# Second projection with half of its value columns last, and the cached values of batch 0 gathered during it

## The reference, cut to what matters

```python
q = einsum('bsd,ed->bse', x, Wq)         # 32 heads of 128
k = einsum('bsd,ed->bse', x, Wk)         # 8 heads of 128
v = einsum('bsd,ed->bse', x, Wv)         # 8 heads of 128
q, k = rope(rmsnorm(q, q_norm_w), pos), rope(rmsnorm(k, k_norm_w), pos)
kc = k_cache[block_table]; vc = v_cache[block_table]   # 512 cached positions for each batch
k_all = concatenate([kc, k], axis=1); v_all = concatenate([vc, v], axis=1)
scores = einsum('bqhd,bkhd->bhqk', q, repeat(k_all)) * SCALE     # masked by cache_seqlens
o = einsum('bhqk,bkhd->bqhd', softmax(scores), repeat(v_all))
return einsum('bse,de->bsd', o, Wo)
```

## Time and profile before

| | |
|---|---|
| median of 3 runs | 1663.63 us (1663.25 to 1664.19) |
| profiled execution, its own time | 1663.88 us |
| span of the profiled execution | 1662.1 us |
| mean granted TensorE clock | 0.992 |
| busy share of the span: PE, DVE, ACT, POOL | 97%, 67%, 57%, 18% |
| second projection, first matmul | 553.85 us |
| cached attention, first matmul | 860.17 us |
| all DMAs issued by POOL (queue q0) | 9216 packets, 67.11 MB |
| all DMAs issued by SP (queue q1) | 220826 packets, 222.90 MB |

### The profile page before, as it was taken

The page is one execution under the profiler, slowest core; times in us unless marked ns, Lnnn a source line. Parts: engine busy times, 40 slices in busy tenths (PEclk is TensorE's granted clock), DMA queues, the critical chain, the costliest instruction groups (busy, mean ns, idle before and its releaser), DMA issues. The chain is left out here.

```text
span 1662.1 us, 33975 instructions
## 1 busy us (share of the span) xinstructions
PE 1604.7 (97%) x10728; PEld 1399.0 (84%) x10728; DVE 1112.0 (67%) x2941; ACT 939.8 (57%) x2392; POOL 303.4 (18%) x306
## 2 busy tenths in 40 slices
PE   2899999999999999999989999999999999999998
PEld 2787888888888788888868999999999999977777
DVE  8404543554346557777777999999999999864443
ACT  3224323232322246676667999999999999822221
POOL 1000000000000146565530211211211211022210
PEclk9999999999999999999989999999999999999999
DMA  6621222202210324434558999999999999595401
GB/s 230 210 96 48 71 70 69 69 0 69 69 63 26 127 100 133 125 117 133 158 176 279 301 321 311 297 324 310 296 325 310 300 318 310 186 316 151 120 7 51
DMA packets 230095, 290.69 MB, mean 175 GB/s; under 512 B 17658, under 2 KB 181914, under 8 KB 221850
## 3 DMA queue, kind: packets, MB, share of 16 engines
q1 hardware_dynamic: 220826, 222.90, 42.7%
q0 software_dynamic: 9216, 67.11, 11.2%
HBM read 237.44 MB, written 50.41 MB: 173 GB/s over the span
## 5 line engine op out<-in xcount | busy, mean ns | idle before, releaser
L1607 PE MATMUL p_val<-probs_t,vals 128*128 128x128 f32 x2048 | 272.2, 276 | 0.3 <-DMA vals<-in_v_pages,rows_now 0.3
L1607 PEld LDWEIGHTS p_val<-probs_t,vals 128*128 128x128 f32 x2048 | 249.5, 192 | 0.7 <-DMA vals<-in_v_pages,rows_now 0.7
L1516 DVE CUSTOM_DVE_ANT_0 probs<-p_score,mask 128x544 f32<-128x544 f32 x256 | 184.3, 720 | 41.9 <-issue 35.8
L1420 ACT ACTIVATE probs<-probs,low 128x544 f32<-128x544 f32 x256 | 190.2, 743 | 0.3 <-DVE low L1516 0.3
L1505 DVE TENSOR_TENSOR wo_lo<-keys,wo_hi 128x544 fp32r<-128x544 f32 x224 | 161.8, 722 | 0.6 <-ACT wo_hi L1415 0.6
L459 PE MATMUL p_tile<-w_hi,y_hi 128*128 128x512 f32 x384 | 157.3, 410 | 2.4 <-PEq L472 2.4
L1428 ACT ACTIVATE probs_t<-p_turn 128x512 f32<-128x512 f32 x256 | 148.9, 582 | 17.4 <-PE p_turn L1586 17.3
L1073 POOL TENSOR_TENSOR w_lo<-w_raw,w_hi 128x512 fp32r<-128x512 f32 x44 | 57.7, 1317 | 550.2 <-DVE w_hi L1111 533.9
L1415 ACT ACTIVATE wo_hi<-keys 128x544 fp32r<-128x544 f32 x224 | 145.8, 651 | 18.2 <-PE p_score L461 17.0
L1586 PE MATMUL p_turn<-cst,probs 128*128 128x128 f32 x1024 | 154.7, 274 | 0.2 <-ACT probs_t L1428 0.2
L459 PE MATMUL p_score<-wo_hi,q_hi 128*128 128x272 f32 x448 | 150.9, 337 | 0.8 <-DVE low L1516 0.4
(11 more groups left out here) (218 smaller groups left out, 3541.7 us busy)
## 6 DMA issues: line engine op xcount, KB each, us to landing
keys<-in_k_pages SPq DMA_DIRECT2D x512, 128.0 KB
qk_new<-x_res SPq DMA_DIRECT2D x80, 256.0 KB, 2.2
x_res<-qk_new SPq DMA_DIRECT2D x32, 512.0 KB
o_new<-x_res SPq DMA_DIRECT2D x32, 512.0 KB, 6.5
w_raw<-in_w_vkq_t SPq DMA_DIRECT2D x12, 1024.0 KB, 5.6
w_raw<-in_w_qkv_t SPq DMA_DIRECT2D x10, 1024.0 KB, 8.4
toep<-kpad SPq DMA_DIRECT2D x32, 256.0 KB, 4.5
w_raw<-in_w_dense_t SPq DMA_DIRECT2D x8, 1024.0 KB, 5.4
```

The lines of the kernel that those rows point to most:

```text
L1420: nc.scalar.activation(probs[:, i % 8, :], probs[:, i % 8, :], ACT.Exp, bias=low[:, i % 4:i % 4 + 1], scale=-1.0, accum_out=total[:, i % 4 ...
L1516: v.tensor_tensor_reduce(out=probs[:, i % 8, :], in0=score_at(i % 2, slice(0, KEYS)), in1=mask[:, i // HK, :], scale=1.0, scalar=3e38, op0 ...
L1607: mm = pe.matmul(p_val[:, h, half * P:(half + 1) * P], vals[:, slot, c // RUN, c % RUN * HK * D + k * D:c % RUN * HK * D + (k + 1) * D], p ...
```

## The change

The weight columns are put in another order: the first half of the values, then keys, queries, and the second half of the values last. So pair 0 is 8 tiles of values and 8 of keys, pairs 1 to 4 hold keys and queries, and pair 5 is 8 tiles of queries and 8 of values. The last three turns now stand between tiles of values. DVE makes the page rows after the angles instead of ahead of them, and the tables for the keys ahead of those for the queries. The cached values of batch 0 get a buffer of their own, `vals_0`, at the other end of SBUF, where nothing of `cached_qkv` lies (`v_out` moves there too), and POOL gathers them ahead of the last pair. SP no longer waits at the end of `cached_qkv` for the stores of the values; it waits for them in `cached_attention`, ahead of its first load of `vals_new`. The diff, cut to its core:

```diff
+    def place_values(self, ctx, nc):
+
+        self.vals_0 = ctx.enter_context(nc.sbuf_tensor("vals_0", [P, GATHERS, RUN * HK * D], F32, side="right"))
+    def gather_values(self, pool, to, slot, done, v_pages):
+
+        v_flat = v_pages.rearrange("o (t r) n -> (o t) (r n)", r=RUN)
+        for n in range(GATHERS):
+            pool.indirect_dma_start(to[:, n, :], None, v_flat, bass.IndirectOffsetOnAxis(ap=self.rows_now[:, slot, n:n + 1], axis=0)).then_inc(done, 16)
...
-        pairs = lambda body, eng: (body(1, True, False), _loop(eng, 2, PAIRS - 1, lambda m: body(m, False, False)),
-                                   body(PAIRS - 1, False, True))
+        TURNED = (QKV_CHUNKS - 2) * TT
+
+        pairs = lambda body, eng: (body(0, True, False), body(1, False, False),
+                                   _loop(eng, 2, PAIRS - 1, lambda m: body(m, False, False)), body(PAIRS - 1, False, True))
+        values = lambda i, first, last: first and i < TT or last and i >= TT
...
+            def store_values(w, i):
+
+                sp.wait_ge(tile_taken, w // TT * TURNED + w + 1)
+                sp.dma_start(v_rows[:, i % TT, w // TT * E:(w // TT + 1) * E], v_out[:, i % 2, :]).then_inc(v_stored[i % 2], 16)
...
+                late = [TT - LAG + i // 2 if i % 2 == 0 else TT + i // 2 for i in range(2 * LAG)]
+                order = [*range(TT - LAG), *late, *range(TT + LAG, PAIR)] if last else range(PAIR)
...
+                    if values(i, first, last):
+                        store_values(i, i)
...
-                    if last and i == TT + 3:
+                    if last and i == 3:
...
-            for i in range(2):
-                sp.wait_ge(v_stored[i], 16 * PAIR // 2)
...
+            def take_values(w, i):
+
+                if w == TT:
+                    act.wait_ge(tile_taken, TT + TURNED)
+                if w >= 2:
+                    act.wait_ge(v_stored[i % 2], 16 * (w // 2))
+                nc.scalar.activation(v_out[:, i % 2, :], p_tile[:, i % 4, :], ACT.Copy).then_inc(tile_taken, 1)
...
+                    if first and i == EC:
+                        act.wait_ge(angles3, 1)
+                        nc.scalar.activation(ang[:, :, :, :], ang[:, :, :, :], ACT.Sin).then_inc(sines3, 1)
                     act.wait_ge(tile_done, m * PAIR + i + 1)
+                    if values(i, first, last):
+                        if last and i - LAG < TT:
+                            put(m, i - LAG)
+                        take_values(i, i)
+                        continue
...
             pairs(body, act)
-            for i in range(PAIR - LAG, PAIR):
-                put(PAIRS - 1, i)
...
+            tables.gather_values(pool, tables.vals_0, 0, tables.vals_gathered_0, io["v_pages"])
             tiles(PAIRS - 1, False, True)
-            rotate(PAIRS - 1, PAIR - 1)
...
-            tables.make_rows(v, cst)
...
+            tables.make_rows(v, cst)
...
-            for which in range(2):
+            for which in (1, 0):
...
+                    if not values(i, first, last):
+                        scale_and_rotate(m, i, 1 if first or isinstance(m, int) and m == 1 and i < TT else 0)
...
-            for i in range(PAIR):
-                project(0, i)
-
             def body(m, first, last):
                 for i in range(PAIR):
                     project(m, i)
-                    if i >= LAG:
+                    if i >= LAG and not values(i - LAG, first, last):
                         turn(m, i - LAG)
-                    elif not first:
+                    elif i < LAG and not first:
                         turn(m - 1, PAIR + i - LAG)
 
-            body(1, True, False)
-            _loop(pe, 2, PAIRS, lambda m: body(m, False, False))
-            for i in range(PAIR - LAG, PAIR):
-                turn(PAIRS - 1, i)
+            pairs(body, pe)
...
-        vals = sb("vals", [P, 2, GATHERS, RUN * HK * D])
+        vals = (tables.vals_0, sb("vals_1", [P, GATHERS, RUN * HK * D]))
...
+                    if first and slot == 0:
+                        for i in range(2):
+                            sp.wait_ge(tables.v_stored[i], 16 * TT)
...
+                    if first and slot == 0:
+                        continue
...
-        "w_vkq_t": lay(np.concatenate([inputs["L0_cond2_Wv"], inputs["L0_cond2_Wk"], inputs["L0_cond2_Wq"]]).T),
+        "w_vkq_t": lay(np.concatenate([wv[:E], inputs["L0_cond2_Wk"], inputs["L0_cond2_Wq"], wv[E:]]).T),
...
+            tables.place_out(ctx, nc)
+            tables.place_values(ctx, nc)
```

More of the change, by code:

```diff
@@ L874, in __init__ @@
         self.qk_stored = [sem(f"qk_stored{i}") for i in range(4)]
+        self.v_stored = [sem(f"v3_stored{i}") for i in range(2)]
         self.pages_ready = sem("pages_ready")
@@ L959, in cached_qkv @@
         tile_taken = sem("tile_taken")
-        v_stored = [sem(f"v3_stored{i}") for i in range(2)]
+        v_stored = tables.v_stored
         squares_ready = sem("squares_ready")
@@ L1060, in body @@
                         put(m - 1, PAIR + i - LAG)
-                    if 1 <= i % TT <= EC and not (last and i >= TT):
+                    if 1 <= i % TT <= EC:
                         split_hi(2 * m + 1 + i // TT, (1 + i // TT) % 2, i % TT - 1)
             pairs(body, act)
-            for i in range(PAIR - LAG, PAIR):
-                put(PAIRS - 1, i)
         @block.gpsimd
@@ L1074, in split_lo @@
                                         ALU.subtract).then_inc(lo_piece, 1)
[L1076 to L1078 removed]
+            for c in range(EC):
+                split_lo(1, 1, c)
             def rotate(m, i):
@@ L1087, in tiles @@
                 for i in range(PAIR):
-                    if i >= 1:
+                    if 1 <= i <= TT and not first or i > TT and not last:
                         rotate(m, i - 1)
-                    elif not first:
+                    elif i == 0 and not first:
                         rotate(m - 1, PAIR - 1)
-                    if 1 <= i % TT <= EC and not (last and i >= TT):
+                    if 1 <= i % TT <= EC and not values(i, first, last):
                         split_lo(2 * m + 1 + i // TT, (1 + i // TT) % 2, i % TT - 1)
-            tiles(1, True, False)
+            tiles(0, True, False)
+            tiles(1, False, False)
             _loop(pool, 2, PAIRS - 1, lambda m: tiles(m, False, False))
@@ L1155, in scale_and_rotate, with tiles @@
                 ins.then_inc(tile_taken, 1)
-            def tiles(m, key):
+            def tiles(m, first, last):
                 for i in range(PAIR):
-                    scale_and_rotate(m, i, key)
-            for c in range(EC):
-                split_hi(2, 0, c)
-            tiles(1, 1)
-            _loop(v, 2, PAIRS, lambda m: tiles(m, 0))
+                    if not values(i, first, last):
+                        scale_and_rotate(m, i, 1 if first or isinstance(m, int) and m == 1 and i < TT else 0)
+            pairs(tiles, v)
         @block.tensor
@@ L1279, in cached_attention @@
         v_new_in = [sem(f"v_new_in{i}") for i in range(2)]
-        vals_gathered = [sem(f"vals_gathered{i}") for i in range(2)]
+        vals_gathered = (tables.vals_gathered_0, sem("vals_gathered1"))
         carrier_ready = sem("carrier_ready")
@@ L1378, in body @@
                     b = 2 * m + slot
+                    if first and slot == 0:
+                        continue
                     if not first:
                         pool.wait_ge(val_done, (b - 1) * HK)
-                    if not (first and slot == 0):
-                        row = pool.snap(b) if not first else b
-                        if not first:
-                            hold_wait(0)
-                        nc.gpsimd.tensor_copy(rows_now[:, slot, :], rows[:, bass.ds(row, 1), :].rearrange("p o n -> p (o n)")).then_inc(rows_placed, 1)
-                        pool.wait_ge(rows_placed, b + 1)
-                        hold_wait(1)
-                    for n in range(GATHERS):
-                        gather(vals[:, slot, n, :], rows_now[:, slot, n:n + 1], v_flat, vals_gathered[slot])
+                    row = pool.snap(b) if not first else b
+                    if not first:
+                        hold_wait(0)
+                    nc.gpsimd.tensor_copy(rows_now[:, slot, :], rows[:, bass.ds(row, 1), :].rearrange("p o n -> p (o n)")).then_inc(rows_placed, 1)
+                    pool.wait_ge(rows_placed, b + 1)
+                    hold_wait(1)
+                    tables.gather_values(pool, vals[slot], slot, vals_gathered[slot], v_pages)
             body(0, True)
```

59 lines of the change are left out of this document (21 added, 38 removed).

## The result

The median of the runs fell from 1663.91 to 1652.28 us (four runs each, one more of the kernel before than in its table): a ratio of 0.9935, interval 0.9924 to 0.9947. I had forecast 1654.0. In the profiles the span went from 1662.1 to 1650.1 us, PE's busy time from 1604.7 to 1598.4.

What follows compares the result with a forecast made beforehand. The prediction took PE's own work to bound the kernel, with losses at the second projection's end, the key wait and the clock; 3.9 + 3.7 + 2.9 - 0.9 = 9.6 us less gave 1654.0 us, range 1652 to 1657.

Steps and rivals of the forecast that it cites:

- The end of the second projection: Last four turns move between tiles of values, so the attention starts at 856.25 instead of 860.17: 3.9 us less.
- The weights: Last chunk's weight load lands late beside batch 0's gathers; ACT is 5.0 us late and PE waits 0.9 us.
- The 88% and the 0.3 us: By the skill's packet rule gathers take some 88% of the DMA; the weight load lands about 0.3 us later still.
- The stage's start: Second projection's start: tables needed sooner, ready near 577.8, with 5.7 us to spare; costed at nothing.
- The keys of batch 1: In the attention, keys land 1.4 us ahead of PE, so PE's key wait goes: 3.7 us less.
- a key wait of some us is left: Sign that the forecast is wrong: PE still waits some us for batch 1's keys.
- the margin of 1.4 us: Batch 1's keys land at 874.7, 1.4 us ahead of PE, which is ready at 876.1.
- Rival (2): Batch 1's keys come over 4 us later than worked out, the key wait stays: 1660.6 us; chance 0.17.
- The clock behind the wait: Batch 1 of the attention takes its steady length at full clock: 2.9 us less, or nothing if the wait stays.
- Rival (1): The clock holds through the attention's first rows, winning 2.0 us more: 1652.0 us; chance 0.10.
- The sum: Whole kernel: 3.9 + 3.7 + 2.9 - 0.9 = 9.6 us less, a median of 1654.0 us.

Runs made afterwards that it cites:

- second profile: The changed kernel run once more, unedited, beside three variants on the same chip: 1652.10 us, ratio 0.9941.
- the kernel with later gathers: The changed kernel, but POOL issues batch 1's gathers only when batch 1's keys have landed: 1649.47 us, ratio 0.992.
- the gather alone: The kernel before, old order of tiles, with batch 0's values gathered in the second projection into a buffer at SBUF's other end: 1656.09 us, ratio 0.9966.
- the later set: Runs of the unedited changed kernel again beside three variants on the same chip: 1652.10 us, ratio 0.9941.
- the kernel with the earlier gathers: The changed kernel, but POOL issues batch 0's two gathers one tile (3.2 us) sooner: 1652.02 us, ratio 0.9934.
- the order alone: The changed kernel, but POOL gathers batch 0's values at the attention's start again, ahead of batch 1's: 1658.25 us, ratio 0.9974.

## Why the prediction was right

- **The end of the second projection, 3.9 us.** Right, and a little short: 4.3 at equal clock. The 5.24 of the two profiles holds also the 1.6 us of the clock at 554, which I had not thought could differ behind the same code, less 0.64 by which the changed kernel's profile came to the second projection later.
- **The weights, -0.9.** Wrong in size: nothing. The step that failed is "Beside the gathers SP's queue moves 0.074 x 7.4 = 0.55 MB": it has the load and the gathers start to flow together, near 807 us in the times of before, 2.6 us after their issue. In the changed kernel the load's data came 1.9 us after its issue and the gathers' 4.6 after theirs, when the load was nearly through. The mechanism itself is real, and so is its cover: one tile earlier the load stands still and ACT waits 3.9 us, with no wait on PE. The 88% and the 0.3 us that I set beside this took SP's mean packet of 1.0 KB for the load's. The load's packets are 2.0 KB (0.33 MB in 163), and the same working then gives 78%, about the row's 79%.
- **The stage's start, nothing.** Right: PE has no wait there, and DVE had 4.3 us to spare (5.7 by my working).
- **The keys of batch 1, 3.7 us.** Mis-sized: 2.4 won, 1.33 (1.94 in the second profile) left, which by my own sign, "a key wait of some us is left", is where I was wrong. My time for the landing was near: 18.45 us after the start by my working, 18.82 and 19.40 measured. In part that is luck: from 858 to 867 the gathers moved their 2.10 MB, and so were through some 12 us after the start where I had 10.45, but SP's queue moved 0.88 MB beside them where I had 0.40. What failed is the other side of "the margin of 1.4 us": PE was ready after 17.49 us, not 19.83, because its first rows ran faster. A gain on one side of a wait had used up the margin on the other. Rival (2) did not come true: the keys landed 0.4 and 0.95 us later than I had worked out, not over 4. The gathers of batch 1 held them up by 3.0 to 3.6 us, as the kernel with later gathers shows, and my working had that in it.
- **The clock behind the wait, 2.9 us.** 2.06 won, where I had nothing if a wait stayed. The clock is at 1.00 in this batch, behind a wait of 1.33 us, but that wait costs 18.81 - 18.02 = 0.8 us more in the rows behind it, as the kernel without it shows.
- **Rival (1), the clock in the first rows.** This came true in good part, 2.34 us (I had given it 2.0, and a chance of 0.10). With the gather alone, in the old order, PE is ready for batch 1 after 19.17 us, 0.66 sooner than before, so the order's clock is the other 1.7. It was not won on top, as the rival had it: with the gather alone batches 0 and 1 gain 6.74 us, with the whole change 6.81, since PE was ready sooner only to wait for the keys. The time came out nearer to the rival's 1652.0 than to 1654.0, but not by its path. My reason against it, that 2.4 us of idle time at 554 had brought 0.72, was a poor one, since the same place shows 1.00 in six of the ten profiles. The half clock still comes, but some 2 us after the first scores (0.50 from 857 to 860), and for some 3 us; in the second profile it lasts nearly 7, and PE is ready after 17.46 us all the same. The Trainium skill, TensorE: Matmul & The Clock Gate, section "HAM oscillation — how this bites in real kernels", lays the fall on idle gaps that are long enough, and by it this rival would have been the forecast. On row 0 the trace agrees: idle times of 1.44 and even 3.19 us left its four matmuls at 1.16 and 1.15. At 554 us it is not enough to go by: behind the same gap of 2.44 us the clock fell in four profiles and stayed up in six.
- **The sum.** Predicted 9.6, measured 11.6 in the medians (11.3 in the later set). The gains from the boundary at equal clock (4.3), batch 0 (4.75) and batch 1 (2.06) make 11.1; the rest is within what the clock at 554 does. Of the 1.5 us above my sum, 0.9 is the weights, 0.4 the boundary and 0.2 the two batches. That batch 0 and 1 together gave 6.8 where I had 6.6 is partly luck: less from the key wait and batch 1, as much more from the first rows.

What brings the clock at 554 to 0.72 or to 1.00, and why the gathers' data follow their issue by 4.6 us beside the weight load, but by 1.8 us in the kernel with the earlier gathers (803.02, first data in 804.8 to 805), was not settled.

## What to carry to other kernels

When a transfer is forecast to come just ahead of its use, work out again when the use itself will be ready: here the same change made PE faster by 2.3 us and left a wait where 1.4 us of margin stood on paper. Where a big gather and small loads that are needed sooner share the DMA engines, order them by hand: one wait on POOL, which holds the gather back until the keys are in, won another 2.6 us, while moving a small load behind the gather cost 3.9. Judge the end of a stage by the trickle of short work as a whole, not by its last gap: without it the first rows of the next stage ran faster too, and PE was ready some 1.7 us sooner. And compare stages from their own first instruction and at equal clock: two profiles alone gave 5.24 us for a step that was worth 4.3.

## What the runs showed of the hardware

- PE at rest for 3.19 us kept its full clock into the next row (1.15 us for four matmuls). Some 8 us of turns with waits between them, of which the longest was 2.54 us, left the next row at half (2.15), and so did a wait of 2.25 us some 12 us into the attention (the order alone: 2.07 us for eight matmuls that take 1.06 later). The length of the last gap does not decide it alone.
- The same code at the same place got 0.72 or 1.00 of the clock in the profiles of different kernels, behind the same gap of 2.44 us, and this moves what follows by 1.6 us.
- Two gathers issued 3.5 us ahead of a weight load left SP's queue nothing from 806.5 to 810, though that load's data came 1.9 us after its issue in the changed kernel. The Trainium skill, DMA: Bandwidth & Descriptors, section "Queues, rings and completion order", has the queues served in turn, packet by packet. By the profile's packets (7.5 KB in q0, 2.0 KB for the load), if they are the page's, that would have left the load a fifth (an estimate); the trace shows nothing of it. Issued 0.3 us before the load instead of 3.5, the gathers came behind it.
